# Lot products of the conv loops as two 48-row products at partitions 0 and 64

## What is computed

```python
def _nnconv(x, src, dst, edge_attr, ew, eb, rw, rb):
    W = (edge_attr @ ew + eb).reshape(edge_attr.shape[0], x.shape[1], rw.shape[1])
    xj = x[src]
    msg = jnp.einsum('ei,eio->eo', xj, W)
    agg = jax.ops.segment_sum(msg, dst, num_segments=x.shape[0])
    return agg + x @ rw + rb
...
h = jnp.maximum(_layernorm(x, axis=-1), 0.0)
x = x + _L0_gnn_ref(h, edge_index, edge_attr_8, ...)      # three _nnconv, D = 16, 8 edge features
h = jnp.maximum(_layernorm(x, axis=-1), 0.0)
x = x + _L1_gnn_ref(h, edge_weight1, ...)                 # segment_max(h[src] * w, dst) @ W.T + b
```

## Time and profile before

| | us |
|---|---|
| runs | 15,849.73, 15,823.62, 15,772.46 |
| median | 15,823.62 |
| profiled execution | 15,828.34 |
| its span, first to last instruction | 15,826.5 |
| mean granted clock of PE, share of the full one | 0.835 |

### The profile page before, as it was taken

The page is one execution under the profiler, slowest core; times in us unless marked ns, Lnnn a source line. Parts: engine busy times, 40 slices in busy tenths (PEclk is TensorE's granted clock), DMA queues, the critical chain, the costliest instruction groups (busy, mean ns, idle before and its releaser), DMA issues.

```text
span 15826.5 us, 172679 instructions
## 1 busy us (share of the span) xinstructions
PE 10936.5 (69%) x49036; PEld 9829.8 (62%) x49036; DVE 6966.9 (44%) x10636; ACT 6831.8 (43%) x6857; POOL 7526.9 (48%) x7820
## 2 busy tenths in 40 slices
PE   4767777677467777777756777677777477777775
PEld 3666666666356666666645666666666477777774
DVE  4444444444344444444444444444444233333332
ACT  2444444444244444444433444444444355555553
POOL 4444444444444444444454444444444555555555
PEclk9888888888688888888877888888888788888887
DMA  2222222222122222222212222222222111111111
GB/s 74 59 58 56 60 59 59 57 59 60 47 58 56 59 60 57 58 60 57 58 47 62 58 58 59 57 59 61 57 57 59 21 27 29 29 28 30 29 28 20
DMA packets 373774, 808.74 MB, mean 51 GB/s; under 512 B 151095, under 2 KB 211264, under 8 KB 373479
## 3 DMA queue, kind: packets, MB, share of 16 engines
q0 software_dynamic: 250112, 432.57, 13.4%
q1 hardware_dynamic: 123623, 375.72, 7.4%
HBM read 676.80 MB, written 130.92 MB: 51 GB/s over the span
## 4 chain that ended last, share of the span: by engine, by line
PE 36%; another core or an unknown queue 34%; issue 18%; DVE 5%; ACT 4%; POOL 2%; ACTq 1%; DVEq 0%; DMA 0%; POOLq 0%; SPq 0%
PE pY L727 31%; PE pY L748 3%; ACT hot_key L611 2%; POOL gathered L549 2%; DVE xe L861 2%; DVE gathered L273 1%; DVE msg L943 1%; PE pY L466 1%; ACT run_pair L829 1%; DVE rows L968 1%; PE pT L737 1%; ACTq L237 1%; ACT apart L606 0%; ACT xeT L799 0%
## 5 line engine op out<-in xcount | busy, mean ns | idle before, releaser
L727 PE MATMUL pY<-part,hot_key 128*128 128x400 f32 x44640 | 9744.4, 380 | 2936.0 <-DVE xe L861 1985.1
L727 PEld LDWEIGHTS pY<-part,hot_key 128*128 128x128 f32 x44640 | 8998.1, 209 | 3440.0 <-DVE xe L861 2111.6
L549 POOL DMA_INDIRECT gathered<-conv_table,idx x5580 | 5354.2, 960 | 6405.5 <-DVE idx L984 4644.8
L606 ACT ACTIVATE apart<-key_pair,zone_lane 128x1408 f16<-128x1408 f16 (+1 forms) x1984 | 2856.6, 1487 | 5185.5 <-remote 4004.3
L861 DVE TENSOR_REDUCE xe<-pY 128x16 f32<-128x400 f32 x5580 | 3087.5, 569 | 4355.7 <-PE pY L727 2244.3
L611 ACT ACTIVATE hot_key<-apart,hot_line 128x1408 fp32r<-128x1408 f16 (+1 forms) x1984 | 3033.2, 1577 | 0.0
L549 POOL DMA_INDIRECT gathered<-max_table,idx x1736 | 1685.0, 971 | 1537.0 <-DVE idx L984 1016.6
L273 DVE TENSOR_TENSOR gathered<-pY,pe_attr 128x432 f32<-128x432 f32 x1488 | 775.5, 563 | 3687.3 <-remote 3491.0
L748 PE MATMUL pY<-edge_w,xeT 96*128 96x432 f32 (+2 forms) x2976 | 1370.7, 589 | 1108.0 <-issue 631.6
L748 PEld LDWEIGHTS pY<-edge_w,xeT 96*128 96x128 f32 (+1 forms) x2976 | 593.4, 214 | 1568.4 <-issue 1534.8
L943 DVE TENSOR_REDUCE msg<-gathered 128x240 f32<-128x2160 f32 x744 | 1558.5, 2095 | 0.2
(11 more groups left out here) (132 smaller groups left out, 1380.3 us busy)
## 6 DMA issues: line engine op xcount, KB each, us to landing
key_pair<-key_rows SPq DMA_DIRECT2D x248, 672.0 KB
scanned<-run_pair SPq DMA_DIRECT2D x248, 416.0 KB
gathered<-conv_table,idx POOLq DMA_INDIRECT x5580
attr_pair<-in_attr SPq DMA_DIRECT2D x186, 208.0 KB
gathered<-max_table,idx POOLq DMA_INDIRECT x1736
key_pair<-key_rows SPq DMA_DIRECT2D x248, 78.0 KB
conv_table<-gathered SPq DMA_DIRECT2D x36, 360.0 KB, 2.2
key_pair<-key_rows SPq DMA_DIRECT2D x744, 6.0 KB
```

Source lines behind the costliest of these rows:

```text
L549: e.indirect_dma_start(out=G[s][:, t, 0:width], out_offset=None, in_=table[:, :], in_offset=bass.IndirectOffsetOnAxis(ap=idx[s][:, t:t + 1 ...
L606: e.activation(apart[k][:, cols], keys[s][:, cols], ACT.Abs, bias=zone_lane[:, z:z + 1]).then_inc(s_abs.sem, 1)
L727: ins = e.matmul(pG[bank], hot_key[s][:, z, at:at + P], part[:, z * NEAR:(z + 1) * NEAR, :], start=(z == 0 and k == 0), stop=(z == ZONES - ...
```

## The change

The two products of a lot no longer share one block-diagonal weight of up to 96 rows. Steps 0 to 2 of a lot stand at columns 0 to 47 of its part of `xe`, steps 3 to 5 at columns 64 to 111, so that after the transpose (112 columns, both lots) they lie on partitions 0 to 47 and 64 to 111 of `xeT`. `edge_w` holds the same three-step block (48 x 432) at partitions 0 and 64. Product q contracts the 48 rows from partition 64q, and in the compiled program it is an instruction for a tile of 64 x 128 of the array at row 0 or 64; before, all were 128 x 128. Banks, columns and the number of instructions are the same. Each product raises s_prod itself, and the waits on it count 4 a chunk. `xe` is filled with zeros once, as columns 48 to 63 and, in lot 1, the last 16 are not written in the conv loops.

```diff
@@ -32,7 +32,11 @@
-PIECES = [[(k, min(3, b - a - k)) for k in range(0, b - a, 3)] for a, b in LOTS]
+TRIO = 3
+PIECES = [[(k, min(TRIO, b - a - k)) for k in range(0, b - a, TRIO)] for a, b in LOTS]
+HALF = 64
+DEEP = TRIO * D
+LOT = HALF + DEEP
...
-        edge_w = sb("edge_w", [TH * D, TH * ROW])
+        edge_w = sb("edge_w", [LOT, TRIO * ROW])
...
-        xe = slots(sb, "xe", [P, TP_KEYS * D])
-        xeT = sb("xeT", [TH * D, P])
+        xe = slots(sb, "xe", [P, 2 * LOT])
+        xeT = sb("xeT", [LOT, P])
...
-        INIT_ALL = 2 + 3 * SLOTS
+        INIT_ALL = 2 + 4 * SLOTS
...
+                e.memset(xe[s][:, :], 0.0).then_inc(s_init.sem, 1)
...
-                e.transpose(pT[0][0:(b - a) * D, 0:P], xe[c[1]][:, a * D:b * D], ident[:, :]).then_inc(s_xt.sem, 1)
+                e.transpose(pT[0][0:LOT, 0:P], xe[c[1]][:, half * LOT:(half + 1) * LOT], ident[:, :]
+                            ).then_inc(s_xt.sem, 1)
...
-                deep = (LOTS[half][1] - LOTS[half][0]) * D
                 for q, (k, m) in enumerate(PIECES[half]):
-                    ins = e.matmul(pE[:, q, 0:m * ROW], xeT[0:deep, :], edge_w[0:deep, k * ROW:(k + m) * ROW],
-                                   start=True, stop=True)
-                ins.then_inc(s_prod.sem, 1)
+                    rows_of = slice(q * HALF, q * HALF + DEEP)
+                    e.matmul(pE[:, q, 0:m * ROW], xeT[rows_of, :], edge_w[rows_of, 0:m * ROW],
+                             start=True, stop=True).then_inc(s_prod.sem, 1)
...
-                gate(e, "act", s_prod, number(c) * 2 + (half + b_prod))
-                deep = (LOTS[half][1] - LOTS[half][0]) * D
-                e.copy(xeT[0:deep, :], pT[0][0:deep, 0:P]).then_inc(s_xeT.sem, 1)
+                gate(e, "act", s_prod, number(c) * 4 + (2 * half + b_prod))
+                e.copy(xeT[:, :], pT[0][0:LOT, 0:P]).then_inc(s_xeT.sem, 1)
...
-                e.tensor_reduce(xe[s][:, j * D:(j + 1) * D], pG[j % BANKS].rearrange("p (r d) -> p d r", d=D),
+                at = j * D
+                if not is_max:
+                    half, k = divmod(j, TH)
+                    at = half * LOT + k // TRIO * HALF + k % TRIO * D
+                e.tensor_reduce(xe[s][:, at:at + D], pG[j % BANKS].rearrange("p (r d) -> p d r", d=D),
...
-                gate(e, "dve", s_prod, number(c) * 2 + (half + 1 + b_prod))
+                gate(e, "dve", s_prod, number(c) * 4 + (2 * half + 2 + b_prod))
...
-        edge_w.append(diagonal(TH, block[:, :ROW], ROW, bias[:ROW])[:-1])
+        trio = diagonal(TRIO, block[:, :ROW], ROW, bias[:ROW])[:-1]
+        edge_w.append(np.concatenate([trio, np.zeros((HALF - DEEP, TRIO * ROW), np.float32), trio]))
```

More of the change, by code:

```diff
@@ L51 @@
 assert CHUNKS % SLOTS == 0 and CHUNKS <= P and LANES * NB == N and DIGITS == 3 and NEAR <= 2 * ZONES * ZONES
-assert TH * D <= P and TP_CONV >= HEAD + 6 and PE_EDGES <= NB * D
+assert TH <= 2 * TRIO and LOT <= P and TP_MAX * D <= 2 * LOT and TP_CONV >= HEAD + 6 and PE_EDGES <= NB * D
 assert W0 * W1 * W2 == EPAD and LOOKS * LOOK == NB and W0 <= P and GB * (W1 + 1) <= 512
@@ L1014, in edges @@
             if not is_max:
-                for cc in (s_xt, s_xeT, s_prod):
+                for cc in (s_xt, s_xeT):
                     bump(cc, 2 * CHUNKS)
+                bump(s_prod, 4 * CHUNKS)
                 bump(s_pe_factors, CHUNKS)
```

## The result

| | before | after |
|---|---|---|
| runs, us | 15,849.73, 15,823.62, 15,772.46, 15,809.44 | 15,372.98, 15,324.54, 15,377.95, 15,465.46 |
| median | 15,816.53 | 15,375.47 |
| ratio, with its 95% interval | | 0.9727 [0.9701, 0.9753] |
| span of the profiled execution | 15,826.5 | 15,371.1 |

The kernel is 441 us, 2.7%, faster. The prediction was no change (15,817 us), its range ended at 15,640. It was wrong, in size and in kind.

The account below looks back on a forecast made before the run. The late signal of the lot products plus the tail behind it was taken to bound conv chunks. Terms -13 - 1 + 0 + 8 + 0 = -6 us gave 15,822 profiled, 15,817 us as median; range 15,640 to 15,980.

Parts of the forecast that it names:

- What bounds the kernel: Conv chunk: the late signal of lot 0's product (17 to 21 us into POOL's burst) plus the tail behind DVE's multiplication.
- the groups' limit: Lot products on TensorE, 1,433 us busy: halving them could never give more than some 700 us, 4.5%.
- The overlap: Lot 1's four passes: partly side by side, 1.20 us to 0.84, gain 0.36, bounds 0 and 0.48.
- The switch: TensorE going from full array to half-array tiles and back: 0.165 us each, 0.33 a lot, bounds 0 to 0.26 each.
- the slower rival: Ahead of the 40 gather products, switches cost more than overlap gives: 15,902 to 16,050 us, chance 0.22.
- Net a lot: Overlap gain less two switches on TensorE: -0.36 + 0.33 = -0.03 us for lot 1, -0.03 for lot 0.
- Lot 0 counted in 35 periods only: Lot 0's product: its signal is late in 331 of 366 periods, so its saving counts in 35: -1 us.
- The slope: Conv chunk: the next index row comes 1.04 us later for each us that lot 0's product starts later, from 267 periods.
- Signals: Each product signals by itself, four a chunk and not two: taken as 0, at most 70 us.
- Transposes and fills: Transposes of 112 columns cost +8 us, bounds 0 and 23; the two start fills on DVE are hidden, 0.
- The overlap works: Rival: lot products overlap and a switch is nearly free, 15,710 or 15,590 us; faster range 15,350 to 15,745, chance 0.30.
- lot 0's half counts in every chunk too: Extension of the faster rival: the signal's delay shrinks with the product, up to 268 us more, 15,350 us.

Follow-up runs that it names:

- Lot 0 alone: The changed kernel with only lot 0 as two 48-row tiles, lot 1 on the whole array: 0.9898 on a quick chip, 15,944.21 us (0.9934) on a slow one.
- the held burst: The changed kernel, with POOL's burst waiting until DVE has multiplied lot 0 of the chunk before: 10,274.11 us; with lot 1's product later too, 10,180.24 us (quick chips).

## Why the prediction was wrong, point by point

**What bounds the kernel** was read rightly for the slow chip. The gain came out of the late signal of the lot products, and the groups' limit (700 us) held.

**The overlap** is the step that failed: "I take the middle ... only the second pass of the first can run beside the first pass of the second". The passes don't go in the order of the program. Both first passes start together; in lot 0 both second ones follow 0.46 us later, in lot 1 the shorter product's second pass comes first. At a spacing of 0.36 us lot 0 takes two spacings fewer, 0.72 us, and lot 1 0.48. The prediction had 0.36 for each, and its upper bounds, 0.48 for lot 1 and full overlap for lot 0, were the truth as far as the overlap goes. The Trainium skill, page "TensorE: Matmul & The Clock Gate", section "Part 3: Packing small matmuls — row/col tiling", states just this, that products on different rows of the array start some 4 ns apart and run at the same time; the trace agrees, with 6 ns. The prediction cited another page for the parallel tiles and took half of what it says.

**The switch** was close. In a stream at full clock the step into a tiled lot grew from 0.183 to 0.275 us. All that lot 0 loses against the overlap of 0.72, with the wider spacing of the pairs in it, is 0.72 - 0.33 = 0.39 us: 0.09 on the way in, 0.10 between the pairs, 0.20 up to the third gather product behind. Two switches at 0.165 were 0.33. In front of lot 1 TensorE often waits for the copy, and part of the switch lies in that wait. So the slower rival was right that the way in and out costs something, but it is less than the overlap gives.

**Net a lot**: predicted -0.03 us each, measured -0.33 (lot 0) and -0.25 (lot 1) on a quick chip. This one term, mis-sized by a factor of about ten, makes 211 us there.

**Lot 0 counted in 35 periods only** was the second step that failed: its length "hardly enters, because its signal is late anyhow". Lot 0 alone brought 103 us on a slow chip where the step has 0.3 x 35 = 11. The passes' position matters in more periods than those that are early already, since a product that comes a little earlier can become early: with both lots 35 became 139. Of this lot 1 has the direct part, as it stands ahead; the last start that is still early hardly moved (6.29 us before, 6.41 after), though the product is 0.6 us shorter.

**The slope** of 1.04 us per us was a straight line through two heaps: of the 267 next index rows, 127 come before 29 us, at 28.1 on average, and 98 after 30.5, at 31.7. A product that starts from 8 us on is nearly always in the later heap, wherever it starts; at the edge of 6.3 us one step of 0.1 us is worth 1.4 us (27.5 for the 18 that start at 6.2 to 6.3, 28.9 for the 57 behind them). After the change the same fit gives 1.23. Applied to the measured shift it would give (0.33 + 0.25) x 1.04 x 372 = 224 us, half of the 441. That the slope gives near TensorE's own time (214 us) is luck, since the line is no mechanism; it missed what the change of heap adds.

**Signals** at 0: right, on both kinds of chip (10,279 against 10,274, 15,342 against 15,358). **Transposes and fills** at +8 us: 10,497 against 10,492, not to be told from 0. **The max stage** unchanged: right.

**The rivals.** "The overlap works" came nearest in mechanism, "lot 0's half counts in every chunk too, up to ... 15,350" nearest in time (15,375). The reason given against it, that the multiplication comes over 21 us in whether the product started at 8 us or later, was true of 146 of those 170 periods (24 start sooner, from 6.5 us) and silent on the 139 whose product started before 7 us; after the change it is 216. The last paragraph had named the sign: the multiplication earlier by more than the product. It moved from 18.65 to 14.53 us on average, the product from 9.13 to 7.54.

## What to carry to other kernels

Where products with a contraction of at most 64 rows follow each other, it is worth trying them on different rows of the array: here a lot of four fp32 passes of 432 columns, with one gather product ahead and two behind it, went from 2.00 to 1.67 us, although going to the tiles and back cost 0.39. Before a slope is taken from a scatter, look whether its points stand in heaps; where a signal either gets through or is held up for 10 us, the worth of a small shift is the share of chunks that change sides, so count how many stand just behind the edge (here 57 of 366 within 0.1 us). And where one engine's signals arrive late, look at what other engine is issuing then: leaving out ten gathers a chunk told that in one run. Before a null result is believed, look whether the edit bit: the held burst on quick chips was held next to never.

## What was not expected of the hardware

- The same program takes 10,483 to 10,492 us on one chip and 15,792 to 16,048 on another, with TensorE's granted clock at 0.963 and 0.835 of the full one on average. On a slow chip the granted clock is 1.00 in the stretch with five gathers, in which TensorE is hardly ever idle, which speaks for the lower clock following the waits and not causing them.
- On a slow chip TensorE's signals are seen up to 13 us late (lot 0's product in the kernel before; 8.7 in the median) while POOL, which issues most of the kernel's DMAs (7,816, SP 1,827), runs through a burst of indirect ones. They come through in steps of 0.70 us, the last some 21.3 us after the burst's first gather. No other engine's are late: where it waited for it, TensorE starts at most 0.13 us behind ACT's copy, and POOL 0.79 us (median) behind DVE's index row, as on a quick chip. The data aren't late either: the last packet ends 2.2 us after the start of a burst's last gather. What the signals and POOL's issues share is open.
- The traces of slow chips also lack records of signals (of the kernel before's, 30% of ACT's and 25% of DVE's; on a quick chip under 2%), so a "remote" there can be a lost record; TensorE's product signals are nearly all there (741 of 744) and themselves late. No run here tells whether taking the profile has a part in this.
- Two passes on tiles of different rows start 6 ns apart, and the next pair of equal ones 0.46 us behind, while whole-array passes follow each other every 0.36 us.
